# The last node layer of a graph network: own products in the edge pass's drain, a new order of products, a mish of three passes, ends per block

## The reference

```python
h = jnp.maximum(_layernorm(x, axis=-1), 0.0)
# layer 3, called with h in the place of x
edge_feat = jnp.concatenate([x[src], x[dst], edge_attr], axis=-1)
h = mish(edge_feat @ W1 + b1)
messages = mish(h @ W2 + b2)
agg = jax.ops.segment_sum(messages, dst, num_segments=x.shape[0])
u = mish(jnp.concatenate([x, agg], axis=-1) @ W3 + b3)
out = u @ W4 + b4
y = x + out
mu = jnp.mean(y, axis=-1, keepdims=True)
var = jnp.mean(jnp.square(y - mu), axis=-1, keepdims=True)
return (y - mu) * jax.lax.rsqrt(var + LN_EPS) * gamma + beta
# mish(x) = x * tanh(softplus(x)); the result is added to the residual x
```

## Time and profile before

| | us |
|---|---|
| median of 3 runs | 2236.05 (2234.85 to 2241.26) |
| the profiled execution's own time | 2239.19 |
| its span, from the first to the last instruction | 2237.5 |
| TensorE busy | 1957.2 |
| VectorE busy | 1573.5 |
| GpSimd busy | 1473.2 |
| ScalarE busy | 1274.9 |
| mean granted clock of TensorE | 0.962 of full speed |
| node layer, first to last TensorE instruction | 2144.06 to 2219.44 |

### The profile page before, as it was taken

How to read it: one execution, slowest core, us unless ns; L and a number is a source line. 1 busy time by engine, 2 the same in 40 slices (tenths; PEclk the granted TensorE clock), 3 DMA queues, 4 the chain that set the end, 5 groups by cost and what they waited for, 6 DMA issues and landing times. The chain is left out here.

```text
span 2237.5 us, 35489 instructions
## 1 busy us (share of the span) xinstructions
PE 1957.2 (87%) x11394; PEld 1133.0 (51%) x11507; DVE 1573.5 (70%) x2245; ACT 1274.9 (57%) x2059; POOL 1473.2 (66%) x1123
## 2 busy tenths in 40 slices
PE   0796887989898769999999978999999999999875
PEld 0775776456565524444444444555555555555432
DVE  8998998633333557777777743888888888888723
ACT  1667777021122246666666633777877777777622
POOL 1787777777600057777777713799889898998530
PEclk9999999989999879999999989999999999999988
DMA  2411001132234234333333204332222222222000
GB/s 117 161 22 46 0 0 43 35 106 60 64 106 113 61 108 140 109 95 93 90 94 90 80 11 128 97 95 76 72 83 72 78 74 71 83 73 77 5 0 23
DMA packets 78495, 165.22 MB, mean 74 GB/s; under 512 B 15999, under 2 KB 41016, under 8 KB 77220
## 3 DMA queue, kind: packets, MB, share of 16 engines
q0 software_dynamic: 34560, 94.69, 15.7%
q1 hardware_dynamic: 43800, 68.78, 9.4%
HBM read 139.86 MB, written 23.39 MB: 73 GB/s over the span
## 5 line engine op out<-in xcount | busy, mean ns | idle before, releaser
L939 PE MATMUL e_two_ps<-w,e_first 128*128 128x512 bf16 x1261 | 382.8, 380 | 4.7 <-issue 0.4
L686 POOL DMA_INDIRECT sorted_records<-edge_record,slot_row x160 | 248.4, 1552 | 69.1 <-issue 54.9
L2371 POOL DMA_INDIRECT e_got<-src_table,e_idx x168 | 225.8, 1344 | 67.2 <-issue 34.1
L939 PE MATMUL e_two_ps<-w,e_first_low 128*128 128x512 bf16 x672 | 255.2, 380 | 0.0
L1707 ACT ACTIVATE u_msg<-u_t,slot_record 128x128 f32<-128x128 f32 x672 | 214.4, 395 | 71.4 <-DVE u_t L1772 71.4
L1888 POOL TENSOR_TENSOR e_first_low<-e_first 128x1024 bf16<-128x1024 f32 x84 | 232.2, 2765 | 19.3 <-DVE e_first L2072 14.9
L1620 POOL TENSOR_TENSOR total<-total,u_part 125x1024 f32 x84 | 198.0, 2357 | 66.9 <-ACT u_part L1715 57.5
L1893 POOL TENSOR_TENSOR e_msg_low<-e_act 128x1024 bf16<-128x1024 f32 x84 | 189.3, 2253 | 39.1 <-DVE e_act L2084 37.7
L1610 POOL DMA_INDIRECT u_got<-up_table,u_idx x168 | 162.0, 964 | 60.0 <-POOL u_idx L1604 32.5
L939 PEld LDWEIGHTS e_two_ps<-w,e_first 128*128 128x128 bf16 x1344 | 128.3, 98 | 141.9 <-issue 2.2
L2079 DVE TENSOR_TENSOR e_lin<-e_two_ps,bias 128x512 f32<-128x512 f32 x168 | 115.3, 687 | 118.4 <-PE e_two_ps L939 118.4
(11 more groups left out here) (373 smaller groups left out, 4725.6 us busy)
## 6 DMA issues: line engine op xcount, KB each, us to landing
conv_w<-in_L_gnn_basis_dram SPq DMA_DIRECT2D x8, 1024.0 KB
sorted_records<-pairs SPq DMA_DIRECT2D x5, 1344.0 KB, 10.4
later_w<-in_L_gnn_W_dram SPq DMA_DIRECT2D x6, 1024.0 KB
attr_parts<-h SPq DMA_DIRECT2D x21, 256.0 KB, 2.1
e_attrT<-attr_parts SPq DMA_DIRECT2D x42, 128.0 KB
e_dst_all<-dst_row SPq DMA_DIRECT2D x42, 125.0 KB
edge_record<-in_edge_floats_dram SPq DMA_DIRECT2D x1, 3125.0 KB
pairs<-in_edge_floats_dram SPq DMA_DIRECT2D x1, 3125.0 KB
```

The costliest lines, as they stand in the source:

```text
L686: pg.nc.gpsimd.indirect_dma_start(out=pg.sorted, out_offset=bass.IndirectOffsetOnAxis(ap=pg.slot_row[:, j:j + 1], axis=0), in_=pg.edge_rec ...
L939: last = nc.tensor.matmul(out, lhsT, rhs, start=(n == 0), stop=(n == len(pairs) - 1))
L2371: pg.nc.gpsimd.indirect_dma_start(out=self.got[:, r * TG + k, :], out_offset=None, in_=table, in_offset=bass.IndirectOffsetOnAxis(ap=self. ...
```

## The change

- **Drain of the edge pass.** For the last two groups (units 80 to 83) the scatter of unit n - 2 stands behind both halves of unit n. The low parts of units 82 and 83 are made by VectorE, right behind `final2`, and no longer by GpSimd.
- **Own products ahead.** Behind the last second layer TensorE computes the own products of blocks 0 to 3 (`own_part`), into the four banks of `pre_ps`, which now live on into the node layer: own products 0 and 1, scatter of 82, own product 2, scatter of 83, own product 3. Block 4's own product is in the node layer.
- **Order in the node layer.** Three turns, then all five products with the sums, then all five second products, which write into the same banks again. Three banks serve the turns of the sums and of u. ScalarE copies the turned u (`take_u`), which VectorE did.
- **Mish in three passes.** The clamp and the Square go; VectorE makes e(e + 2) (`widen`), ScalarE takes a Ln and an Exp with a scale, as the edge pass does. A memset of a constant at the kernel's start goes.
- **Ends per block.** Statistics, root and factors are made for each block behind its second product, and the result of block b - 1 follows the statistics of block b.

```diff
             def low_of_second(n, u):
+                if n >= UNITS - 2:
+                    return
...
             def scatter(n, g, r, u):
-                pe.wait_ge(low2, n + 1 + 2)
+                if n < UNITS - 2:
+                    pe.wait_ge(low2, n + 1 + 2)
+                else:
+                    pe.wait_ge(last_low2, n + 3 - UNITS)
...
+            def own_part(b):
+                ps = pre_ps[b // 2][0:BN, b % 2, :]
+                for f in range(4):
+                    nc.tensor.matmul(ps, pg.hT[:, f, nodes_of(b)], later.big[:, 0, f, :], start=(f == 0), stop=False)
+
             def body(n, g, r, u, at):
                 second_layer(n, g, r, u, 0)
-                if at >= 1:
+                if 1 <= at < NG - 2:
                     scatter(n - 2, g - 1, (r - 1) % RING, u)
                 second_layer(n, g, r, u, 1)
+                if at >= NG - 2:
+                    scatter(n - 2, g - 1, (r - 1) % RING, u)
                 if ahead_of(at):
                     first_layer(n + AHEAD, g + 2, (r + 2) % RING, u)
 
...
-            for u in range(2):
-                scatter(UNITS - 2 + u, NG - 1, (NG - 1) % RING, u)
+            pe.wait_ge(mish1_ready, UNITS + 2)
+            pe.wait_ge(later.tail_in, 16 * TAIL_LOADS)
+            own_part(0)
+            own_part(1)
+            scatter(UNITS - 2, NG - 1, (NG - 1) % RING, 0)
+            own_part(2)
+            scatter(UNITS - 1, NG - 1, (NG - 1) % RING, 1)
+            own_part(3)
...
+                if n >= UNITS - 2:
+                    dve.wait_ge(mish2_ready, n + 1 + 2)
+                    dve.wait_ge(scattered, n - 1 + 2)
+                    nc.vector.tensor_tensor(msg_low[:, u, :, :], act2[:, u, :, :], upper(act2[:, u, :, :]),
+                                            ALU.subtract).then_inc(last_low2, 1)
...
+        turn_ps = [ctx.enter_context(nc.psum_tensor(f"tail_turn{n}", [P, 4, P], FP32)) for n in range(3)]
+        last_ps = ctx.enter_context(nc.psum_tensor("tail_last", [P, D], FP32))
+        node_ps = [pre_ps[b // 2][0:BN, b % 2, :] for b in range(NB - 1)] + [last_ps[0:BN, :]]
...
             def first(b):
...
                 pe.wait_ge(taken, b + 1)
                 for f in range(4):
-                    last = nc.tensor.matmul(u_ps[b % 2][0:BN, :], totalT[:, b % 2, f, :], later.big[:, 1, f, :],
+                    last = nc.tensor.matmul(node_ps[b], totalT[:, b % 3, f, :], later.big[:, 1, f, :],
                                             start=False, stop=(f == 3))
                 last.then_inc(made, 1)
 
-            def second(b):
+            def turn_u(b):
                 pe.wait_ge(mished, b + 1)
-                if b >= 2:
-                    pe.wait_ge(u_taken, b - 1)
+                if b < 3:
+                    pe.wait_ge(taken, b + 3)
+                else:
+                    pe.wait_ge(u_taken, b - 2)
                 for f in range(4):
-                    last = nc.tensor.transpose(u_turn_ps[b % 2][:, f, 0:BN], u[:, b, f * P:(f + 1) * P],
+                    last = nc.tensor.transpose(turn_ps[(NB + b) % 3][:, f, 0:BN], u[:, b, f * P:(f + 1) * P],
                                                pg.ident[0:BN, 0:BN])
                 last.then_inc(u_turned, 1)
-                if b >= 2:
-                    pe.wait_ge(summed, b - 1)
+
+            def second(b):
                 pe.wait_ge(u_taken, b + 1)
...
+                pe.wait_ge(biased, b + 1)
+                accumulate(nc, node_ps[b], [(uT[:, b % 2, f, :], later.big[:, 2, f, :])
+                                            for f in range(4)]).then_inc(out_made, 1)
+
+            for b in range(3):
+                turn(b)
+            for f in range(4):
+                nc.tensor.matmul(node_ps[NB - 1], pg.hT[:, f, nodes_of(NB - 1)], later.big[:, 0, f, :],
+                                 start=(f == 0), stop=False)
+            for b in range(NB):
                 first(b)
-                second(b - 1)
-            second(NB - 1)
+                if b + 3 < NB:
+                    turn(b + 3)
+                elif b >= 3:
+                    turn_u(b - 3)
+            for b in range(NB):
+                second(b)
+                if b + 2 < NB:
+                    turn_u(b + 2)
...
+            def take_u(b):
+                act.wait_ge(u_turned, b + 1)
                 if b >= 2:
...
+                    act.wait_ge(out_made, b - 1)
+                nc.scalar.copy(uT[:, b % 2, :, :], turn_ps[(NB + b) % 3][:, :, 0:BN]).then_inc(u_taken, 1)
+
+            def grow(b):
+                act.wait_ge(biased, b + 1)
+                nc.scalar.activation(e[:, b, :], u[:, b, :], ACT.Exp).then_inc(grown, 1)
+
+            def share(b):
+                act.wait_ge(widened, b + 1)
+                nc.scalar.activation(e[:, b, :], e[:, b, :], ACT.Ln, scale=LOG_SCALE,
+                                     bias=pg.log_bias[0:BN, 0:1]).then_inc(logged, 1)
+                act.wait_ge(logged, b + 1)
                 nc.scalar.activation(e[:, b, :], e[:, b, :], ACT.Exp, scale=-1.0,
...
+                                     bias=pg.share_bias[0:BN, 0:1]).then_inc(shared, 1)
+
+            def spread(b):
+                act.wait_ge(var, b + 1)
+                nc.scalar.sqrt(sd[:, b:b + 1], sd[:, b:b + 1]).then_inc(root, 1)
+
+            def norm(b):
+                act.wait_ge(scaled, b + 1)
+                nc.scalar.activation(e[:, b, :], e[:, b, :], ACT.Identity, bias=nmr[:, b:b + 1],
+                                     scale=rs[:, b:b + 1]).then_inc(normed, 1)
+
+            for b in range(3):
+                take(b)
+            for b in range(NB):
+                grow(b)
+                if b >= 3:
+                    take_u(b - 3)
+                share(b)
+                if b + 3 < NB:
+                    take(b + 3)
+            for b in range(NB):
                 if b + 2 < NB:
...
+                    take_u(b + 2)
+                spread(b)
+                norm(b)
...
+            def bias(b):
                 dve.wait_ge(made, b + 1)
...
+                nc.vector.tensor_tensor(u[:, b, :], node_ps[b], b3, ALU.add).then_inc(biased, 1)
+
+            def widen(b):
+                dve.wait_ge(grown, b + 1)
+                nc.vector.scalar_tensor_tensor(out=e[:, b, :], in0=e[:, b, :], scalar=2.0, in1=e[:, b, :],
+                                               op0=ALU.add, op1=ALU.mult).then_inc(widened, 1)
+
+            def mish(b):
                 dve.wait_ge(shared, b + 1)
+                dve.wait_ge(biased, b + 1)
                 nc.vector.scalar_tensor_tensor(out=u[:, b, :], in0=e[:, b, :], scalar=1.0, in1=u[:, b, :],
                                                op0=ALU.subtract, op1=ALU.mult, reverse0=True).then_inc(mished, 1)
...
 
             def rest(b):
                 dve.wait_ge(out_made, b + 1)
                 dve.wait_ge(h_ready, b + 1)
                 dve.wait_ge(mished, b + 1)
-                link(nc.vector.tensor_tensor(e[:, b, :], out_ps[b % 2][0:BN, :], pg.h[:, b, :], ALU.add))
-                dve.sem_inc(summed, 1)
+                link(nc.vector.tensor_tensor(e[:, b, :], node_ps[b], pg.h[:, b, :], ALU.add))
                 link(nc.vector.bn_stats(out=stats[:, b, :], in_=e[:, b, :]))
                 link(nc.vector.bn_aggr(out=mv[:, b, :], in_=stats[:, b, :]))
...
+                nc.vector.tensor_scalar(sd[:, b:b + 1], mv[:, b, 1:2], EPS, None, ALU.add).then_inc(var, 1)
+                dve.wait_ge(root, b + 1)
+                link(nc.vector.reciprocal(rs[:, b:b + 1], sd[:, b:b + 1]))
+                nc.vector.scalar_tensor_tensor(out=nmr[:, b:b + 1], in0=mv[:, b, 0:1], scalar=-1.0,
+                                               in1=rs[:, b:b + 1], op0=ALU.mult, op1=ALU.mult).then_inc(scaled, 1)
 
...
+            bias(0)
+            for b in range(NB):
+                widen(b)
+                if b + 1 < NB:
+                    bias(b + 1)
+                mish(b)
+            for b in range(NB):
+                rest(b)
+                if b >= 1:
+                    result(b - 1)
+            result(NB - 1)
```

More of the change, by code:

```diff
@@ L2512, in turn @@
             def turn(b):
-                if b >= 2:
-                    pe.wait_ge(taken, b - 1)
+                if b >= 3:
+                    pe.wait_ge(taken, b - 2)
                 for f in range(4):
-                    last = nc.tensor.transpose(turn_ps[b % 2][:, f, 0:BN], total[:, b, f * P:(f + 1) * P],
+                    last = nc.tensor.transpose(turn_ps[b % 3][:, f, 0:BN], total[:, b, f * P:(f + 1) * P],
                                                pg.ident[0:BN, 0:BN])
@@ L2550, in _ @@
-            first(0)
-            for b in range(1, NB):
-                first(b)
-                second(b - 1)
-            second(NB - 1)
+                pe.wait_ge(biased, b + 1)
[6 more added lines that the diff above has]
+                                 start=(f == 0), stop=False)
@@ L2566, in take @@
```

(52 more changed lines are left out.)

60 lines of the change are left out of this document (12 added, 48 removed).

## The result

The changed kernel takes 2186.2 us (median of 4 runs, 2185.7 to 2190.4) where the kernel before takes 2237.1: the ratio is 0.9775, 95% interval 0.9755 to 0.9794. That is 50.9 us less by the medians, against 45.2 forecast, and inside the range by 0.2 us. The profiled execution has a span of 2184.4 us, 53.1 less than before.

What follows compares the result with a forecast made beforehand. TensorE, busy 87% of a 2237.5 us span, was taken as the bound; 8.6 us gained up to the node layer plus 36.6 in it made 45.2, so 2236.05 us became 2190.9, range 2186 to 2198.

Steps and rivals of the forecast that it cites:

- The drain as TensorE's list: Edge pass drain: TensorE's halves, scatters and own products sum to 37.1 us from 2097.25, ending at 2135.1 with waits.
- The wait ahead of unit 82: Drain: TensorE waits for low halves of unit 83's first layer, taken as 0.5 us, bound 1.4.
- VectorE's slack in the drain: Drain: VectorE's work is ready before each scatter is due; for scatter 83, at 2128.9 against 2130.6.
- The barrier: Between edge pass and node layer: GpSimd's drain over early, node layer starts 0.3 us behind TensorE's end, at 2135.4.
- (B): Rival at the barrier: it costs 2.6 us behind whoever is last, GpSimd's drain being no cause; 2193.2 us, chance 0.13.
- The node layer: TensorE's list of 42.4 us plus 5.6 behind the last product: 48.0 us against 84.6, 36.6 gained.
- (C): Rival in the node layer: copies of u make ScalarE reload its table, twice 1.28 us a block; 2193.7 us, chance 0.08.
- (D): Rival in the node layer: turns behind the barrier bring a 1.2 GHz stretch; 2192.6 us, with a second 2194.4, chance 0.12.
- (E): Rival in the drain: it is still a chain, TensorE idles 3 to 6 us more; 2194 to 2197 us, chance 0.10.
- (F): Rival: clock drops to 1.2 GHz at the first own product and stays, 51 us more; 2242 us, chance 0.02.
- The clock: Changed order: no hole over 1 us, so 2.4 GHz throughout; 1.7 us more if transposes do not count as busy.
- The stores: Kernel's end: stores and final barrier behind VectorE's last instruction stay at 8.84 us.

Runs made afterwards that it cites:

- the first experiment: The kernel before with the drain's new order and VectorE's low halves, old node layer, no own products ahead: 2228.6 us, ratio 0.9951.
- experiments 1 and 2: New drain order before the old node layer, no own products ahead, against the kernel before: last low halves on VectorE 2228.6 us, on GpSimd 2227.1 us.
- experiment 5: The changed kernel with the last two low halves back on GpSimd: median 2190.5 us beside 2188.1 of the changed kernel.
- Experiment 4: The changed kernel with own products 0 to 3 back in the node layer, behind the turns: 2202.0 us, ratio 0.9833 to the kernel before.

## Why the prediction was right, point by point

- **The drain as TensorE's list: right.** Forecast 8.6 us gained up to the first turn, measured 8.8; by the windows, 46.81 us before and 38.05 after, for 38.1 forecast. The wait ahead of unit 82 was 0.4 us (by the step of 0.22 from 2100.81 the next matmul was due at 2101.03 and started at 2101.44; 0.25 us of it show as idle), forecast 0.5.
- **VectorE's slack in the drain: right in its result, with one term missing.** The widen of unit 82 stood for 1.7 us behind GpSimd's low halves, a contention that the prediction did not have. Scatter 83 had 1.7 us of slack in the forecast (due at 2130.6, VectorE ready at 2128.9), thanks to the own products in front of it. In the trace 1.5 are left: the addition that it waits for ends at 2123.27, and it starts at 2124.76, behind own product 2. Most of the delay ended ahead of that, in a bias that VectorE had to wait for anyway, as in the first experiment. The Trainium skill ("SBUF — State Buffer", SBUF: two separate sides) describes this as an exclusive lock between the two engines, held for a whole instruction, by whichever starts first, where the VectorE instruction has two inputs in SBUF; the trace agrees, since the widen ended 1.08 us behind GpSimd (2111.78 against 2110.70), a little less than the 1.22 it takes alone.
- **The barrier: right, (B) refuted.** 0.30 us behind TensorE; GpSimd's drain 7.07 us and a bound of its own only where nothing else covers it, as the drains of experiments 1 and 2 show. The 2.3 us that the prediction puts down to GpSimd's drain are no share of the low halves' move, though: with them back on GpSimd (experiment 5) the first turn comes no later.
- **The node layer: right.** Forecast 48.0 us, measured 47.7; last product 42.3 for 42.4. No second table load of ScalarE that reached the path (C), no stretch at 1.2 GHz behind the turns (D), no chain in the drain (E), no fall of the clock (F).
- **The clock: right, and worth more than the prediction said.** In the changed kernel it stays at 1.00. Behind the barrier and three turns in a row the products are at 3.43 to 3.45, so the 1.7 us that the rule of the Trainium skill ("TensorE: Matmul & The Clock Gate", Part 4: PE-mode transpose) would have cost did not come. This does not refute the rule: barrier and turns are 1.8 us in all, less than the idle times of 3.0 and 4.8 us behind which the lower clock showed. Experiment 4 shows the other side: with the holes of the drain open, 2.7 us go to the lower clock.
- **The stores: wrong.** "Stores and final barrier stay at 8.84 us": they took 7.2. The step failed by taking the time behind VectorE's last instruction as fixed, where it was the rest of a burst of 1.28 MB. With the burst kept it is 8.8, 10.3, 10.6 and 10.8 us in four kernels, so that the gain was 1.7 us between these two profiles and would be nearer 3.4 us against the slower bursts.
- **Upstream: not in the prediction.** It counted the memset at nothing, which stays open. 5.8 us lie between the two profiled executions, some 5 of which one kernel also shows between executions of its own. With the 1.7 us of the stores this put the median at the edge of the range: that it stayed inside, by 0.2 us, is luck, while the 45.2 us of the forecast and the 45.7 measured in its part are not. A range of 1 us each way was too narrow, since 14 executions of the changed kernel spread over 8.7 us.

The shares, from the anchor: new order 10.8, VectorE's low halves 1.1, the new order of the node layer with the ends per block 20.4 (84.6 to 64.1), own products moved 13.4; together 45.7. The first two are counted in the drain alone, the third in the layer alone; taken one by one to VectorE's last end, the changes gained 10.8 (new order alone), 9.4 (the new drain) and 18.6 us (the new layer behind the old drain). The unchanged stage was not the same each time, at other granted clocks: 87.1 us of old layer for 84.6, 51.7 of old drain for 49.9. Of the 20.4, 3.7 are the results between the statistics, and none is mish.

## What to carry to other kernels

When the last stage starves TensorE twice, in the drain ahead of it and in the chain within it, look for independent products of the next stage whose operands are already there and put them into the holes: the work disappears, and here the clock stayed up for what followed. Sum such a stage as one engine's list, then check each joint for slack and the other engines for their total per block. Count stores at the end as bytes by rate from the first one on, not as a fixed tail, and allow for a spread ahead of the changed part as large as the runs of one kernel show.

## What the runs showed of the hardware that was not expected

- GpSimd's drain at the end of the edge pass lasts 7.07 us from the start of its last operation of 1.89 us, in every kernel, whatever the other engines do; at the end of the node layer it is over 0.1 us behind its last operation (12.26 us from 2144.4 for operations that end at 2156.5, in the kernel before). What the 5.2 us are is not shown.
- A VectorE operation of two SBUF operands that started just behind a GpSimd one took 2.91 us instead of 1.22, and in the node layer one took 1.84 instead of 0.69 beside GpSimd's additions. The other way round, GpSimd's low halves took 2.89 us instead of 1.89 where VectorE's widen had started 0.08 us ahead (2131.85 and 2131.93 before): this is the 2.89 in the old loop.
- Splitting the last stores over two queues changed nothing: the rate was 99 and 100 GB/s for 99 and 94, and the DMA engines' share 0.32 and 0.26 for 0.33 and 0.26.
